# One indirect transfer at a time: a wait for landing behind each of GpSimd's 256 scatters and gathers

## The reference, cut to what matters

```python
x = x + gnn(layernorm(x), adj, ...)        # LN, adj @ h, two 128x128 weights, relu, residual
x = x + ffn(layernorm(x), ...)

# ffn
gate = x @ Wg.T + bg                        # (rows, 8)
scores, idx = top_k(gate, 2)
combine = sum(softmax(scores)[..., None] * one_hot(idx, 8), axis=-2)
for e in range(8):
    h = relu(x @ W1[e].T + b1[e])           # 128 -> 512
    y = h @ W2[e].T + b2[e]                 # 512 -> 128
    out = out + combine[..., e:e+1] * y
```

## Time and profile before

| | |
|---|---|
| median of 3 runs | 627.26 us |
| lowest, highest | 627.03 us, 627.95 us |
| profiled execution, first to last instruction | 878.1 us |
| granted TensorE clock in it, mean | 0.761 |
| indirect transfers | 128 scatters, 128 gathers |
| packets of the queue that carries them | 8192, 16.79 MB |

### The profile page before, as it was taken

How to read it: one execution, slowest core, us unless ns; L and a number is a source line. 1 busy time by engine, 2 the same in 40 slices (tenths; PEclk the granted TensorE clock), 3 DMA queues, 4 the chain that set the end, 5 groups by cost and what they waited for, 6 DMA issues and landing times.

```text
span 878.1 us, 14976 instructions
## 1 busy us (share of the span) xinstructions
PE 471.1 (54%) x4776; PEld 395.1 (45%) x4777; DVE 385.6 (44%) x1146; ACT 237.7 (27%) x467; POOL 272.6 (31%) x268
## 2 busy tenths in 40 slices
PE   0613243441799997401099997201299951899500
PEld 0613233330688886201088886100188840688400
DVE  2979933830454667200044668000055620456622
ACT  0413100210356554000056553000044410344200
POOL 3053373067000000777400001777300067000274
PEclk9955575565799999655589999655599975899955
DMA  9980012011112112211112112111122222221341
GB/s 346 416 287 1 19 51 64 6 58 51 43 44 78 56 57 67 68 54 51 33 44 78 57 57 82 52 54 51 27 73 72 72 78 53 74 73 54 135 132 57
DMA packets 32173, 70.78 MB, mean 81 GB/s; under 512 B 14458, under 2 KB 14714, under 8 KB 31364
## 3 DMA queue, kind: packets, MB, share of 16 engines
q1 hardware_dynamic: 21520, 37.66, 13.0%
q0 software_dynamic: 8192, 16.79, 6.6%
q10 hardware_dynamic: 2420, 15.77, 4.4%
HBM read 32.45 MB, written 37.75 MB: 80 GB/s over the span
## 4 chain that ended last, share of the span: by engine, by line
PE 42%; issue 20%; another core or an unknown queue 13%; DVE 13%; DMA 4%; ACT 3%; POOL 3%; SPq 2%; ACTq 0%; DVEq 0%; POOLq 0%
PE PH L876 14%; PE PY L893 13%; PE PH L872 5%; POOL YG L311 3%; DMA ADJ<-in_adj 3%; PE PX L859 2%; ACT N L695 1%; PE PY L886 1%; SPq L223 1%; ACT N L677 1%; PE PA L824 1%; DVE VARN L377 1%; DVE MDIF L376 1%; DVE N L442 1%
## 5 line engine op out<-in xcount | busy, mean ns | idle before, releaser
L298 POOL DMA_INDIRECT rows<-XHL,IDX x128 | 123.2, 962 | 347.1 <-DVE IDX L515 309.3
L540 DVE SCALAR_TENSOR_TENSOR HL<-PH,HH 128x512 f16<-128x512 f32 x192 | 129.8, 689 | 207.0 <-ACT HH L726 114.1
L726 ACT ACTIVATE HH<-PH 128x512 f16<-128x512 f32 x192 | 113.6, 596 | 263.1 <-PE PH L876 107.9
L311 POOL DMA_INDIRECT YG<-yrows,IDX x128 | 121.3, 948 | 202.7 <-DMA yrows<-YB 164.3
L876 PE MATMUL PH<-XT,W1H 128*128 128x256 f16 x768 | 144.3, 281 | 22.8 <-issue 22.6
L893 PE MATMUL PY<-W2H,HL 128*128 x768 | 131.0, 223 | 31.8 <-issue 31.8
L893 PE MATMUL PY<-W2H,HH 128*128 x768 | 131.1, 223 | 25.3 <-issue 25.3
L893 PE MATMUL PY<-W2L,HH 128*128 x768 | 109.3, 223 | 42.1 <-issue 42.1
L535 DVE COPY XT<-PX 128x512 f16<-128x512 f16 x96 | 40.5, 422 | 168.6 <-issue 63.1
L876 PE MATMUL PH<-XT,W1L 128*128 128x256 f16 x384 | 107.8, 281 | 12.3 <-issue 12.3
L876 PEld LDWEIGHTS PH<-XT,W1H 128*128 x768 | 76.3, 100 | 55.8 <-issue 32.9
(11 more groups left out here) (154 smaller groups left out, 559.8 us busy)
## 6 DMA issues: line engine op xcount, KB each, us to landing
rows<-XB ACTq DMA_DIRECT2D x4, 3072.0 KB, 29.8
XB<-rows SPq DMA_DIRECT2D x32, 384.0 KB
yrows<-YB SPq DMA_DIRECT2D x32, 384.0 KB, 2.3
out<-X SPq DMA_DIRECT2D x16, 256.0 KB
X<-in_x SPq DMA_DIRECT2D x3, 1024.0 KB, 28.2
YG<-in_w ACTq DMA_DIRECT2D x1, 2048.0 KB, 9.6
ADJ<-in_adj SPq DMA_DIRECT2D x32, 64.0 KB, 3.8
YG<-in_w SPq DMA_DIRECT2D x1, 2048.0 KB, 29.7
```

What stands on the lines that cost most here:

```text
L298: nc.gpsimd.indirect_dma_start(rows[q], bass.IndirectOffsetOnAxis(ap=IDX[:, col:col + 1], axis=0), XHL[:, src:src + 2 * P].bitcast(F32), N ...
L311: nc.gpsimd.indirect_dma_start(YG[q % 2][:, dst:dst + P], None, yrows[q], bass.IndirectOffsetOnAxis(ap=IDX[:, col:col + 1], axis=0)).then_ ...
L540: nc.vector.scalar_tensor_tensor(HL[:, at:at + 2 * BW], PH[h][:, :], 0.0, HH[:, at:at + 2 * BW], ALU.max, ALU.subtract).then_inc((loa_made ...
L726: nc.scalar.activation(HH[:, at:at + 2 * BW], PH[h][:, :], ACT.Relu).then_inc((hia_made, hib_made)[h][j], 1)
```

## The change

Behind every indirect transfer stands a wait of POOL for that transfer's own data:

```diff
                         nc.gpsimd.indirect_dma_start(
                             rows[q], bass.IndirectOffsetOnAxis(ap=IDX[:, col:col + 1], axis=0),
                             XHL[:, src:src + 2 * P].bitcast(F32), None).then_inc(scattered[q], 16)
+                        pool.wait_ge(scattered[q], (t * 2 + k + 1) * 16)
...
                         nc.gpsimd.indirect_dma_start(
                             YG[q % 2][:, dst:dst + P], None, yrows[q],
                             bass.IndirectOffsetOnAxis(ap=IDX[:, col:col + 1], axis=0)).then_inc(gathered[q][t // GT], 16)
+                        pool.wait_ge(gathered[q][t // GT], (t % GT * 2 + k + 1) * 16)
```

## The result

The changed kernel takes 898.74 us (median of 4 runs, 893.14 to 898.97) where the kernel before takes 627.14 us: a ratio of 1.4289, with a 95% interval of 1.4227 to 1.4351. Repeated later beside the kernel before it was 896.26 against 628.21 us, ratio 1.4276 (1.4233 to 1.4319). The forecast was 869, in a range of 790 to 960. The span of the profiled execution is 897.1 us and its own time 898.95, so 1.85 us lie around it.

The account below looks back on a forecast made before the run. PE's passes were taken to set the pace, except where POOL ends waits ahead of quarter 3 and in the tail. Serial transfers, 188 periods on the path, moved the rebuilt end from 618.7 to 860.2: 627.3 + 241.5 = 869 us, range 790 to 960.

Parts of the forecast that it names:

- The profile's 251 us are not in the timed run: Five stretches of back-to-back POOL transfers lose some 246 us to a standstill, taken as belonging to the profiled execution only.
- The period: Start to start on POOL, landing plus 0.30 us: 2.55 us a scatter, 2.74 a gather, instead of 1.26.
- bounds of 2.36 and 3.8: Lower and upper limits in us for the period of a serial transfer, since no row shows one.
- rival (a): POOL wakes slowly from each wait, or load and store traffic lies on every transfer: 0.45 us more a period, 954 us; chance 0.11.
- Scatter 0 on the path, scatter 1 hidden: Scatter 0 delays DVE's entry into quarter 0 to 186.6 us, 28 later; scatter 1 ends at 264.5, before it is wanted.
- Scatter 2 and gather 0, scatter 3 and gather 1 in one chain: On POOL, gather 0 starts only after scatter 2, so DVE stands 81 us ahead of quarter 2; scatter 3 and gather 1 follow.
- Gather 2 hidden, "just": Gather 2 runs from 673.3 to 761.0 us beside quarter 3, whose last store comes at 761.4.
- the 8.6 I carried: The 8.6 us of the median above the rebuilt 618.7: what lies around a span and what the rebuilding misses.
- step 5: Quarter 3's routing lies behind DVE's wait: scatter 3 starts at 504.0, gather 1 reaches DVE at 673.1, DVE stands 102 us.
- (b): The transfer latency is partly the profiler's, like the standstill: a period of 2.2 us, 784 us; chance 0.08.
- (c): Faster: the standstill is real and engines go on between transfers; at a 1.4 us period 592 us; chance 0.03.
- (d): The waits are passed at once or are hidden, 627 us; chance 0.02.

Follow-up runs that it names:

- split_wait_serial: The changed kernel, with DVE entering quarters 2 and 3 after the first 8 of 32 gathers and waiting for the other 24 after the first pass: 878.65 us.
- nearly unchanged kernel: The kernel before, with waits only behind the 32 scatters of quarter 1 and the first 24 gathers of quarter 2: 630.55 us, ratio 1.0025.
- double stores: The changed kernel with a second 384 KB store, into a spare tensor, behind each of the 32 stores of expert results: 914.61 us.

## Why the prediction was right

The direction, the mechanism and the size were right; 30 of 272 us were missing. Step by step:

- **The profile's 251 us are not in the timed run.** Right, and the largest decision of the prediction. Its reason was only half right: I put the standstill down to the profiled execution. Executions with a profile on the quiet chip have none (628.7 us of span), and on the other chip every execution of the kernel before took 877 to 885 us. So the profile of the kernel before shows a state that none of the first timed runs was in. What differs between the chips isn't known.
- **The period.** 2.55 and 2.74 forecast; 2.50 and 2.73 measured as medians of scatters 0 and gathers 3. The bounds of 2.36 and 3.8 were not needed. The 0.30 us ahead of the next start held as well: a landing of 2.2 us and a period of 2.50 leave no room for rival (a)'s 0.75.
- **Scatter 0 on the path, scatter 1 hidden.** Right: DVE's second copy at 187.76 us (186.6 forecast), and scatter 1 ended at 275, 47 us before its successor.
- **Scatter 2 and gather 0, scatter 3 and gather 1 in one chain, with the routing behind DVE's wait.** Right. DVE enters quarter 2 at 501.1 (485.4) and quarter 3 at 699.8 (673.1), and the split wait showed the gap of 20.8 us to be the only thing that the wait itself costs.
- **Gather 2 hidden, "just".** Wrong, the one step that failed. It was to end at 761.0 beside stores that end at 761.4; it ran until 800.5, and gather 3 followed it and not the last store.

The missing time, from the starts of the groups (measured less forecast): up to scatter 2 +6.0 us, scatter 2 +7.0, gather 0 and the routing +3.0, scatter 3 +7.3, gather 1 +3.1, gather 2 in place of the last store +9.7, the tail +0.8. Together +36.9 on the span; 6.8 fewer lie around it than the 8.6 I carried (1.85): 30.1 us, which is 898.95 less the 868.8 that was rounded to 869.

The first term, the +6.0 us, has nothing to do with POOL. Scatter 0 ended on time, but from DVE's second copy in quarter 0 to that quarter's last store it took 116.7 us (187.76 to 304.48) where 112.1 were reckoned: the first pass took 35.0 us up to its second store, the later ones 27.3. The nearly unchanged kernel has the same, 117.8 us (155.81 to 273.58). So it belongs to both kernels; the rebuilt time before had missed it as well, and it had gone into the 8.6 us. That these two terms, +6.0 and -6.8, nearly cancel is luck.

The other 30.9 us go back, all but some 0.6 us of the routing, to one mis-sized term: I took every period as a quiet one. Beside expert work some are 3 to 5 us long. The first gather after scatter 2 is the plainest, issued when SP at last gets its loads and a store out:

```profile
410.70 0.35 SPq L220 DMA_DIRECT2D XB<-rows  x1
411.09 0.44 SPq L245 DMA_DIRECT2D yrows<-YB  x1
411.57 0.43 SPq L220 DMA_DIRECT2D XB<-rows  x1
...
575.07 0.35 SPq L245 DMA_DIRECT2D yrows<-YB  x1
608.75 0.33 SPq L220 DMA_DIRECT2D XB<-rows  x1
609.13 0.42 SPq L245 DMA_DIRECT2D yrows<-YB  x1
```

That gather needed 5.0 us (410.90 to 415.93 on POOL). The same rows show what I had not followed: SP's store waits in its queue behind a load that waits for all of scatter 2, and scatter 3 later does the same (33 us there). It moved no end, since DVE waited longer in both places; but it is why DVE waits 81 us ahead of quarter 3 and not the 102 of the prediction's step 5. The double stores back traffic as the cause of the long periods, with the reserve that the changed kernel ran on the other chip.

- **Rivals.** (a) fell as a slow wake-up but lives as traffic, with 0.1 us on the average of the 188 periods (20.5 us on the path) instead of 0.45. (b), (c) and (d) fell: the periods are those of the profile, on both chips. But (c)'s mechanism, engines that go on between transfers with one under way, is real on the chip with the standstill: it made waits behind scatter 1 alone worth 33 us. There the changed kernel itself was not run. An estimate: split_wait_serial's 878.65 us plus the 20 of its gap are 899, near 2% more than 880.

The Trainium skill's fixed cost of about 2.0 us per transfer ("DMA: Bandwidth & Descriptors", anatomy of one DMA) gave the prediction's estimate of a landing of 2.15 us and a period of 2.45. The scatters' landing of 2.2 us and their period of 2.50 nearly agree; the gathers' 2.5 and 2.73 are 0.3 us above it.

## What to carry to other kernels

A transfer's price has two parts, the time that the issuing engine spends on it and the latency until it has landed. One under way at a time pays both each time, two pay almost only the first (31 scatters: 39, 41 and 86 us with many, two and one). What that costs a kernel is the number of such periods on the path: count them group by group, and look at a group that is "just" hidden as if it were not, at the periods that it has beside other traffic.

When a profile is much longer than the timed runs, find the stretches that hold the difference, count their work at the undisturbed rate, and see whether what is left over makes up the difference. A comparison of the two spans here, 878 and 897 us, would have said 2%; the runs say 43.

## What the runs showed of the hardware that was not expected

- In two sets of runs, both on one chip, transfers that POOL issues back to back bring PE, DVE and ACT nearly to a halt: 87 matmuls in 39 us beside 32 gathers, where 600 in 55 us are done undisturbed. On another chip, some minutes later, a nearly unchanged kernel runs 901 in 80 us beside 64 of them. The kernel before takes 880 and 628 us there. The cause is open.
- A wait for each transfer's landing, which leaves POOL idle for 1.5 us each time, removes the halt with as many transfers (933 matmuls in 87 us). With two under way it mostly remains (123 in 82 us). Whether the pause does it or the empty queue was not tested.
- An indirect transfer of 64 KB lands 2.2 us (scatter) and 2.5 us (gather) after its start when it is alone, on both chips, and up to 5.1 us beside three transfers of 384 KB, on the quiet chip.
